# Self attention in runs of two slots, with three-product projections, full tile shapes and paired value visits

## The reference

```python
def _L1_ffn_ref(x, Wq, Wkv, Ws, Wo, bo):
    s = jax.nn.sigmoid(x @ Ws)
    vals, idx = jax.lax.top_k(s, TOPK)
    scores = jnp.zeros_like(s).at[bi, ti, idx].set(vals)
    q = (x @ Wq).reshape(b, t, H, DH).transpose(0, 2, 1, 3)
    kv = (x @ Wkv).reshape(b, t, 2, H, DH).transpose(2, 0, 3, 1, 4)
    k, v = (kv[0], kv[1])
    attn = jax.nn.softmax(jnp.einsum('bhid,bhjd->bhij', q * scale, k), axis=-1)
    out = jnp.einsum('bhij,bhjd->bhid', attn, v)
    proj = jnp.einsum('bhtd,hde->bhte', out, Wo) + bo[None, :, None, :]
    return jnp.einsum('bhte,bth->bte', proj, scores)
...
    x = x + _L1_ffn_ref(_layernorm(x, axis=-1), ...)
```

## Time and profile before

| | us |
|---|---|
| median of 3 runs | 2458.72 (2457.88 to 2459.5) |
| the profiled execution: its own time | 2457.71 |
| its span | 2455.7 |
| of that the gates stage, about | 1487 to 1559 |
| start-up of self attention, about | 1559 to 1625 |
| its loop of 8 batches, about | 1625 to 2425 |
| PE busy, whole span | 2085.7 (85%) |
| DVE busy | 1471.1 (60%) |
| granted clock of PE, mean | 0.92 |

### The profile page before, as it was taken

How to read it: one execution, slowest core, us unless ns; L and a number is a source line. 1 busy time by engine, 2 the same in 40 slices (tenths; PEclk the granted TensorE clock), 3 DMA queues, 4 the chain that set the end, 5 groups by cost and what they waited for, 6 DMA issues and landing times. The chain is left out here.

```text
span 2455.7 us, 38024 instructions
## 1 busy us (share of the span) xinstructions
PE 2085.7 (85%) x11977; PEld 1378.2 (56%) x11977; DVE 1471.1 (60%) x2334; ACT 918.0 (37%) x1568; POOL 884.1 (36%) x801
## 2 busy tenths in 40 slices
PE   5760499999999972799999997389999999999997
PEld 2660499999999970333333337145555455555454
DVE  7840244554555443799998875356575666656655
ACT  4520133333333420366666662122232332323332
POOL 0057723551555013455453330113333333333322
PEclk9955799999999985799999995699999999999998
DMA  6572233323332234244443333233232322323231
GB/s 226 203 295 103 79 119 125 113 79 130 118 120 68 78 96 123 77 127 131 126 125 113 111 108 131 58 83 74 61 91 65 86 61 61 94 63 84 65 77 49
DMA packets 155315, 257.46 MB, mean 105 GB/s; under 512 B 25414, under 2 KB 74606, under 8 KB 151914
## 3 DMA queue, kind: packets, MB, share of 16 engines
q1 hardware_dynamic: 111778, 176.24, 25.0%
q0 software_dynamic: 15328, 44.61, 5.5%
q10 hardware_dynamic: 28160, 35.99, 4.5%
HBM read 124.81 MB, written 75.43 MB: 82 GB/s over the span
## 5 line engine op out<-in xcount | busy, mean ns | idle before, releaser
L1207 DVE TENSOR_REDUCE ca_negmax<-ca_na 128x2 f32<-128x1024 f32 x272 | 330.8, 1220 | 42.1 <-PE ca_na L935 39.7
L1057 ACT ACTIVATE ca_pr<-ca_st 128x512 f32<-128x512 f32 x512 | 279.3, 599 | 131.8 <-PE ca_st L949 130.2
L680 DVE TENSOR_TENSOR ex_h<-ex_up,ex_sg 128x512 f32<-128x512 f32 x136 | 94.0, 692 | 306.0 <-ACT ex_sg L643 198.7
L1839 DVE TENSOR_REDUCE sa_negmax<-sa_na 128x1 f32<-128x512 f32 x272 | 182.7, 674 | 132.5 <-PE sa_na L1659 127.9
L935 PE MATMUL ca_na<-ca_k_stack,ca_q_stack 64*128 64x512 f32 x544 | 212.0, 467 | 23.8 <-DVE ca_negmax L1207 21.0
L603 PE MATMUL ex_gp<-ex_xp,moe_gu_p 128*128 128x256 f32 x1632 | 222.2, 286 | 1.6 <-DVE ex_xp L666 1.4
L949 PE MATMUL ca_st<-ca_q_stack,ca_k_stack 64*128 64x512 f32 x512 | 205.7, 462 | 18.0 <-ACT ca_pr L1057 17.4
L616 PE MATMUL ex_yp<-moe_dn_p,ex_hp 128*128 128x256 f32 x1632 | 209.3, 286 | 11.9 <-DVE ex_hp L670 11.9
L603 PE MATMUL ex_up<-ex_xp,moe_gu_p 128*128 128x256 f32 x1632 | 218.1, 283 | 0.0
L1827 POOL TENSOR_TENSOR sa_acc<-sa_acc,sa_pr 128x1024 f32<-128x1024 f32 x64 | 151.6, 2368 | 170.2 <-ACT sa_pr L1778 170.2
L1823 POOL TENSOR_TENSOR sa_acc<-sa_pr 128x1024 f32<-128x1024 f32 x32 | 75.2, 2349 | 381.6 <-ACT sa_pr L1778 381.6
(11 more groups left out here) (284 smaller groups left out, 3786.4 us busy)
## 6 DMA issues: line engine op xcount, KB each, us to landing
sa_q<-sa_qh SPq DMA_DIRECT2D x140, 128.0 KB
sa_k<-sa_kh SPq DMA_DIRECT2D x140, 128.0 KB
ex_raw_m<-masks ACTq DMA_DIRECT2D x34, 512.0 KB, 3.7
moe_gu_raw<-gateupT POOLq DMA_DIRECT2D x8, 2048.0 KB, 8.3
ca_k_stack<-cross_k SPq DMA_DIRECT2D x216, 64.0 KB
ca_q_stack<-cross_q SPq DMA_DIRECT2D x216, 64.0 KB
expert_rows<-rt_zeros SPq DMA_DIRECT2D x20, 512.0 KB, 15.4
cross_q<-ca_qp SPq DMA_DIRECT2D x10, 1024.0 KB, 5.1
```

Of the source, the lines that this page charges most:

```text
L1057: act.activation(pr[:, s // HG % 2, s % HG, :], st[s % 2][:, :], ACT.Exp, scale=DK ** -0.5).then_inc(exp_done, 1)
L1207: dve.tensor_reduce(negmax[:, g % 2, 1 - r % 2, :, r // 2], na[r % 2][:, :, :], AX.X, ALU.max, negate=True).then_inc(max_done, 1)
L1839: dve.tensor_reduce(negmax[:, par, h, t:t + 1], na[s % 2][:, :], AX.X, ALU.max, negate=True).then_inc(max_done, 1)
```

## The change

The eight slots of a unit are taken in four runs of two: both `score_b` of the run, then both `score_a`, with places for jobs between and behind them (12 places: 3r between, 3r+1 behind score_a, 3r+2 behind the values). `values` comes twice a unit with two key tiles each: in run 0 tiles 2 and 3 of the unit before, in run 2 tiles 0 and 1 of this one. The projections are computed as three FP32R products (high x high, high x low, low x high) for which `self_gates` now makes high and low parts of x and of the weights: `normed_T` and so each load of xT are twice as large, 1 MB. A v job makes two key tiles for two pairs of heads in place of four tiles for one. `max_rows` uses a stationary tile of 128 x 128 FP32R that is zero but for two columns; `gparts`, `sel2` and the bias `bo3` are filled up to 128 rows, and the bias product is FP32R. The split of the maxima moves from DVE to POOL. The core of the diff:

```diff
             m.sem(n) for n in ("st_ready", "stats_ready", "std_ready", "rstd_ready", "eps_set", "w_in"))
         gh_ready, gl_ready = m.sem("gh_ready"), m.sem("gl_ready")
+        xh_ready, xl_ready, wh_ready, wl_ready, bo_put = (m.sem(n) for n in ("xh_ready", "xl_ready", "wh_ready", "wl_ready", "bo_put"))
+        x_put = [m.sem(f"x_put{i}") for i in range(2)]
         block = ctx.enter_context(nc.Block())
         @block.gpsimd
         def _(pool):
-            for w, name in weights[:-1]:
-            pool.dma_start(w[:, :], io[name]).then_inc(w_in, 16)
-            pool.wait_ge(w_in, 16 * len(weights))
+            for n in weights:
+                pool.dma_start(raw[n][:, :, :], io[n].rearrange("(c p) n -> p c n", p=P)).then_inc(w_in, 16)
+            pool.dma_start(bo[:, :], io["sbo"]).then_inc(w_in, 16)
+            pool.dma_start(wo[:, :, :], io["sWo"].rearrange("(c p) n -> p c n", p=P)).then_inc(w_in, 16)
+            pool.memset(bo3[:, :].bitcast(F32), 0.0).then_inc(wl_ready, 1)
+
+            def low(b):
+                pool.wait_ge(xh_ready, b + 1)
+                pool.tensor_tensor(xp[:, b % 2, 1, :, :], xt[:, :, b * S:(b + 1) * S], xp[:, b % 2, 0, :, :].bitcast(F32), ALU.subtract).then_inc(xl_ready, 1)
+
+            for b in range(2):
+                low(b)
+            for i, n in enumerate(weights):
+                pool.wait_ge(wh_ready, i + 1)
+                pool.tensor_tensor(weights[n][:, 1, :, :], raw[n][:, :, :], weights[n][:, 0, :, :].bitcast(F32), ALU.subtract).then_inc(wl_ready, 1)
+                low(b + 1 + i)
+            pool.wait_ge(wh_ready, 4)
+            pool.tensor_tensor(bol[:, :], bo[:, :], boh[:, :].bitcast(F32), ALU.subtract).then_inc(wl_ready, 1)
+            for b in range(5, B):
+                low(b)
+            pool.wait_ge(w_in, 16 * 5)
...
+                if t % TB == TB - 1:
+                    b = t // TB
+                    act.wait_ge(xt_ready, t + 1)
+                    if b >= 2:
+                        act.wait_ge(x_put[b % 2], 16 * (b // 2))
+                    act.copy(xp[:, b % 2, 0, :, :], xt[:, :, b * S:(b + 1) * S]).then_inc(xh_ready, 1)
+                    if b == 1:
+                        act.wait_ge(w_in, 16 * 5)
+                        for n in weights:
+                            act.copy(weights[n][:, 0, :, :], raw[n][:, :, :]).then_inc(wh_ready, 1)
+                        act.copy(boh[:, :], bo[:, :]).then_inc(wh_ready, 1)
...
-            if g == 1:
-                JOBS += [("q", g, 0, 1), ("k", g, 1, 1), ("sum", g, 2, 1), ("o0", g, 2, 1), ("v", g, 3, 1), ("o1", g, 4, 1)]
-            else:
-                JOBS += [("q", g, 0, 1), ("k", g, 1, 1), ("sum", g, 2, 1), ("v", g, 3, 1)]
-            JOBS += [("m0", g, 4, 1), ("m1", g, 5, 1), ("gate", g, 6, 1)]
-        FIRST = ["q", "k", "v"] * 3 + ["m0", "m1"]
+            JOBS += {0: [("q", 0, 0), ("k", 0, 2), ("v2a", 0, 4), ("sum", 0, 5), ("v2b", 0, 6), ("m0", 0, 7), ("m1", 0, 9), ("gate", 0, 10)],
+                     1: [("q", 1, 0), ("k", 1, 2), ("o0", 1, 4), ("sum", 1, 5), ("o1", 1, 6), ("m0", 1, 7), ("m1", 1, 9), ("gate", 1, 10)],
+                     2: [("q", 2, 0), ("k", 2, 2), ("v0a", 2, 4), ("sum", 2, 5), ("m0", 2, 6), ("m1", 2, 7), ("gate", 2, 9)],
+                     3: [("q", 3, 0), ("k", 3, 2), ("v0b", 3, 4), ("sum", 3, 5), ("m0", 3, 6), ("m1", 3, 7), ("gate", 3, 9)]}[g]
+        FIRST = ["q", "k"] * 3 + ["v0a", "v0b", "m0", "m1"]
         LAST = ["sum", "gate", "o0", "o1"]
+        TERMS = ((0, 0), (0, 1), (1, 0))
...
-                sp.dma_start(xT[:, :, :], xT_d.rearrange("(c p) n -> p c n", p=P)[:, :, bass.ds(n, S)]).then_inc(xT_in, 16)
+                sp.dma_start(xT[:, :, :, :].bitcast(F32), xT_d.rearrange("(r c p) n -> p r c n", r=2, p=P)[:, :, :, bass.ds(n, S)]).then_inc(xT_in, 16)
...
-                    last = pe.matmul(misc[H:H + 2, t * P:(t + 1) * P], parts[:, par, h, t, :], ident[:, :], start=True, stop=True)
+                    last = pe.matmul(misc[:, t * P:(t + 1) * P], parts[:, par, h, t, :], identr[:, :], start=True, stop=True)
...
+            def project(n, name, c, b):
+
+                bank_free(n)
+                if name[0] == "v":
+                    c0, lo = int(name[1]), "ab".index(name[2]) * 2
+                    for t in range(2):
+                        tok = (lo + t) * P
+                        for i in range(KC):
+                            for wr, xr in TERMS:
+                                last = pe.matmul(misc[:, t * D:(t + 1) * D], xT[:, xr, i, tok:tok + P], weights["sWv"][:, wr, i, c0 * P:(c0 + 2) * P],
+                                                 start=(i == 0 and (wr, xr) == TERMS[0]), stop=(i == KC - 1 and (wr, xr) == TERMS[-1]))
+                else:
                     if name == "q":
                         pe.wait_ge(xT_in, b * 16 + 16)
-                if name == "v":
-                    for t in range(piece * TB // count, (piece + 1) * TB // count):
-                        for i in range(KC):
-                            last = pe.matmul(misc[:, t * P:(t + 1) * P], xT[:, i, t * P:(t + 1) * P], wv[:, i, c * P:(c + 1) * P],
-                                             start=(i == 0), stop=(i == KC - 1))
-                else:
-                    w = wq if name == "q" else wk
-                    for i in range(piece * KC // count, (piece + 1) * KC // count):
-                        last = pe.matmul(misc[:, :], w[:, i, c * P:(c + 1) * P], xT[:, i, :], start=(i == 0), stop=(i == KC - 1))
-                if piece == count - 1:
-                    last.then_inc(misc_full, 1)
+                    w = weights["sWq" if name == "q" else "sWk"]
+                    for i in range(KC):
+                        for wr, xr in TERMS:
+                            last = pe.matmul(misc[:, :], w[:, wr, i, c * P:(c + 1) * P], xT[:, xr, i, :],
+                                             start=(i == 0 and (wr, xr) == TERMS[0]), stop=(i == KC - 1 and (wr, xr) == TERMS[-1]))
+                last.then_inc(misc_full, 1)
...
-                    last = pe.matmul(out, gT[:, tok:tok + P], bo[:, :], start=False, stop=True)
-                if 1 in pieces:
-                    last.then_inc(misc_full, 1)
+                    last = pe.matmul(out, gparts[:, tok:tok + P], bo3[:, :], start=False, stop=True)
...
-                    for s in range(SLOTS):
-                        if s == 0:
+                    for r in range(TB):
+                        if r == 0:
                             pe.wait_ge(misc_free, b * nj + (nf if g == 0 else nf + next(n for n, j in enumerate(JOBS) if j[:2] == ("m1", g - 1)) + 1))
-                        score_b(g, s, u)
-                        score_a((g + 2) % C, b if g < 2 else b + 1, s, u + 2)
-                        if s == 1:
+                        for s in (2 * r, 2 * r + 1):
+                            score_b(g, s, u)
+                        jobs(g, 3 * r, b)
+                        for s in (2 * r, 2 * r + 1):
+                            score_a((g + 2) % C, b if g < 2 else b + 1, s, u + 2)
+                        jobs(g, 3 * r + 1, b)
+                        if r == 0:
                             pe.wait_ge(exp_done, u * TB + 2)
-                            values((g - 1) % C, TB - 1)
-                        if s >= 3 and s % 2:
-                            t = s // 2 - 1
-                            pe.wait_ge(exp_done, u * TB + (t + 3))
-                            if t == 0:
-                                pe.wait_ge(av_free, u + 1)
-                            values(g, t)
-                        for name, piece, count in pieces_at(g, s):
-                            n = job(b, g, name)
-                            if name[0] == "m":
-                                max_rows(n, u + 1, (g + 1) % 2, int(name[1]))
-                            elif name == "sum":
-                                sums(n, u)
-                            elif name == "gate":
-                                if g == 1:
-                                    pe.wait_ge(gT_in, b * 32 + 32)
-                                gates(n, (g - 1) % C)
-                            elif name[0] == "o":
-                                output(n, b, int(name[1]), (0, 1) if count == 1 else (piece,))
-                            else:
-                                project(n, name, (g + 3) % C, b if g == 0 else b + 1, piece, count)
+                            for k in (2, 3):
+                                values((g - 1) % C, k)
+                        elif r == 2:
+                            pe.wait_ge(exp_done, u * TB + 4)
+                            pe.wait_ge(av_free, u + 1)
+                            for k in range(2):
+                                values(g, k)
+                        jobs(g, 3 * r + 2, b)
...
+                    for r in range(TB):
+                        act.wait_ge(st_full, u * TB + (r + 1))
+                        act.wait_ge(av_done, u * TB + (r + 1))
```

(34 more changed lines are left out.)

172 lines of the change are left out of this document (92 added, 80 removed).

## The result

| | before | after |
|---|---|---|
| median (runs) | 2458.3 us (4) | 2362.9 us (4) |
| lowest to highest | 2455.2 to 2459.5 | 2360.0 to 2366.0 |
| span of the profiled execution | 2455.7 | 2362.5 |
| mean granted clock | 0.92 | 0.916 |

The ratio is 0.9614, with a 95% interval of 0.9597 to 0.9631: 95 us faster. The forecast was 2355, 103 us faster.

What follows compares the result with a forecast made beforehand. PE's own instruction stream was taken to bound the loop. Loop −106, gates stage +2.9, start-up +2.3 and tail −2.1 gave −103 from 2458.7: 2355 us, range 2335 to 2395, likeliest case 2345 to 2370 (0.63).

Steps and rivals of the forecast that it cites:

- q and k, v: Loop projections as FP32R instructions: q and k −2.6 us a pass (eight jobs), v −1.1 (four jobs).
- The row jobs: Maximum rows in the loop: four FP32R instructions at 0.11 us replace eight FP32; with edges −1.37 a unit, −5.5 a pass.
- The gate: Gate job in the loop gets a full tile: 0.42 + 0.21 us becomes 0.23, −1.6 a pass.
- Outputs: Output jobs in the loop: two bias products each fall from 0.63 to 0.12 us, −2.0 a pass for both jobs.
- The values: Four values visits a unit become two of double length; eight dropped a pass save 2.9 us, taken as −2.7.
- Waits for the bank: Loop waits for the one misc bank: 6.3 us a pass against 4.2 in the old order, so +2.1.
- The rival that each job waits 0.5 us more: Loop rival: bank costs 0.5 us more on four jobs of each unit, 64 us, 2380 to 2420; chance 0.15.
- The gates stage: Before the loop: +3.3 us for copies in a row, +1.6 for other batches and last copy, −2 for one transfer fewer.
- The start-up: Before the loop: POOL's memset 1.80 us, cheaper q and k give 1.1 back, v0b waits; +2.3 (0 to +5).
- The tail: Behind the loop: one more values pair, but four bias products fall from 3.1 to 0.8 us; −2.1.
- xT: Loop rival: the 1 MB load, 5.8 us with spare 1.8, lands late, 2365 to 2387; chance 0.08.
- the clock: Loop rival: idle gaps drop PE to 1.2 GHz for a share f; about 2690 at f = 0.5; chance 0.03.

Runs made afterwards that it cites:

- rows_fp32_narrow: The changed kernel with the maximum rows back to FP32 and a two-column stationary tile; ratio to the kernel before 0.9713, pass 90.33 us against 87.68.
- jobs_spread: The changed kernel with only job places moved, `sum` behind the next two score_b slots; ratio to the kernel before 0.9449, median 2320.8 us.
- weights_late: The changed kernel with POOL making the weights' low parts behind those of all eight x batches; ratio to the kernel before 0.9616, pass 87.69 us.
- slots_alternate: The changed kernel with score_b and score_a alternating slot by slot inside each run; ratio to the kernel before 0.9867, mean pass 94.85 us.

## Why the prediction was right, point by point

- **Sum and sign.** 2355 was forecast and 2362.9 measured, inside the likeliest case's own span. The loop was to carry nearly all of it and did: −98.2, with −93.1 in the spans as a whole. By the spans 10 us of the forecast's 103 are missing, and they hold errors of both signs: the loop gave 8 less, the gates stage cost 3 more and the start-up 1, and the tail gave 3 more, which is luck.
- **q and k, v.** Priced −3.7 us a pass, from 1.72 to 1.39 and from 1.71 to 1.44. Undoing them cost 3.9. Measured were 1.36 for q (1.48 where it stands behind a wait) and 1.43 for v (1.52 up to a tile of another shape); k is 1.51, since it follows a values visit, and that edge was counted at 0.09 to 0.11.
- **The row jobs.** The form that no row of before showed, priced at 0.11 for each instruction, came out at 0.10 (0.40 a job). The old form (rows_fp32_narrow) is 1.19 a unit longer by starts (0.47 for m0 and 0.72 for m1), not 1.37: the edge between m0 and the values visit was counted though it stays. Undone alone, the edit costs less than that again, 0.5 to 0.8 a unit, because the wait of 0.43 to 0.48 in each unit goes.
- **The gate.** −1.6 priced, 0.64 undone: in units 0 and 1, where it stands behind the wait of 0.43, undoing it costs nothing.
- **Outputs.** Priced at 4.08 a job, measured 3.69 (1929.27 to 1932.96 with the last bias). The missed part is that the 8-row product also lengthened the eight instructions ahead of it.
- **The values.** The edges that two dropped visits save, 2.7 a pass, were taken for a gain. The step failed in what it left out: a visit is also the work that covers an evacuation (the read-out of the bank). Undone, the pass is 3.4 shorter, not 2.7 longer. It did not spoil the forecast because the waits that stood in the place of the visits had been counted, under another heading.
- **Waits for the bank.** 6.3 placed by hand, 5.7 in the list. The places and the lengths are those forecast (0.82 for 0.75 before `sum`, 0.97 for 1.06 behind o0, 0.56 to 0.6 for 0.4 to 0.5 behind the exponential). Behind the gate, at q and at the start of a unit, 0.5 is listed where 0.6 was placed with o1 to m0 in it. The rival that each job waits 0.5 us more (2380 to 2420) falls.
- **What the loop missed.** A pass is 87.68 instead of 86.9, 6 us in all. (The four units of the forecast, 21.1, 26.6, 19.5 and 19.6, add up to 86.8.) Units 0 and 3 are 0.36 and 0.45 longer than forecast, 1 and 2 within 0.16. Four k at 1.51 instead of 1.39 are +0.5, two q at 1.48 are +0.2 and the outputs −0.8; the rest was not split further.
- **The gates stage.** +4.7 with the memset was forecast, +8.0 measured. The step that failed is "POOL's 11 subtractions (2.37 each) spread over the stage": they were given no price, though the rule that POOL and a DVE cast exclude each other stood a few lines above and was used for the maxima alone. With POOL's weight subtractions moved out of the way 2.95 of the 3.3 by which the stage overran came back.
- **The start-up.** +1.7 against +0.5. PE waits 1.05 us for POOL's split before the first `m1`, and both v jobs run at 2.9 us, at half clock. But the figure holds chance: in jobs_spread and weights_late, with the same instructions there, the start-up is 50.9 and 51.0 us at a mean granted clock of 0.82 and 0.83, where the changed kernel has 55.3 at 0.67. So the +1.7 is not shown to be the change's.
- **The tail.** −5.2 instead of −2.1. From the first output to the end are 14.2 us instead of 19.4. Before, two groups of eight ran at half clock (3.75 and 3.78); after, the first one alone does (3.34), so part of the gain is a higher clock, which the forecast did not count; and each is shorter by the edge of the bias.
- **xT, POOL's split, the clock.** 1 MB landed 5.3 us after issue (5.8 was forecast), and PE has no wait for it in the loop. Twice the bytes took 1.7 more; the 2.1 of transfer in the forecast was an assumption that no row showed. POOL's four small operations are 0.20 us each, some 3 us into the unit. The clock stays at 1.00. None of these rivals came about; that the clock can fall when the loop waits longer, slots_alternate shows, at a cost of 5 us and not of hundreds.

The order in which the change takes the slots was not priced as a term of its own. slots_alternate shows that the changed kernel would lose 57 us without it: the wait behind the exponential would be near 1.4 us instead of 0.5. That is not a share of the loop's 98, since the kernel before takes its slots one by one as well and waits only 4 us a pass, with its jobs in other places. How much of the 98 the order is worth against the kernel before is not shown. Undone one at a time in the new order, the other edits (narrow FP32 rows, gate, bias, projections, split, four visits) add up to 6.7 of the 12.4 us by which a pass got shorter. The rest lies in how they meet the waits and the order, and no kernel here has the old order with the new shapes.

## What to carry to other kernels

When all small jobs go through one buffer, cost a job by two numbers: its own length, and the time from its end until the buffer is read out, with whatever stands before the read-out on that engine. A job whose successor waits for something else than the job itself costs nothing to lengthen, as far as it stays inside the wait, and gains nothing when shortened; first put needed work between it and its successor. Here that placing alone, with no instruction changed, gave 41 us; the cheaper projections give 31.

When work moves to GpSimd, look at what VectorE runs in the same microseconds, in every stage that it is moved to, not only in the one that the change is about.
